# Attention stage: the softmax division moved from the weights to a head's output, with the reciprocals sent through DRAM to become a row

## The reference

```python
q = (query @ wq).reshape(bs, sq, N_Q_HEADS, D_K).transpose((0, 2, 1, 3))
...
q = _apply_rope(q, curr_seq_pos)
k = _apply_rope(k, curr_seq_pos)
raw = jnp.einsum('bhqd,bhkd->bhqk', q, k) / scale
masked = raw + mask[:bs, None, curr_seq_pos:curr_seq_pos + sq, :sk]
attn = jax.nn.softmax(masked, axis=-1)
out = jnp.einsum('bhqk,bhkd->bhqd', attn, v)
```

## Time and profile before

| | us |
|---|---|
| median of three runs | 3483.4 |
| lowest run | 3466.51 |
| the profiled execution | 3467.62 |
| its span, first to last instruction | 3465.7 |
| attention stage, from the first scores to the last matmul with v | 1004 to 1972 of the span |

### The profile page before, as it was taken

The page is one execution under the profiler, slowest core; times in us unless marked ns, Lnnn a source line. Parts: engine busy times, 40 slices in busy tenths (PEclk is TensorE's granted clock), DMA queues, the critical chain, the costliest instruction groups (busy, mean ns, idle before and its releaser), DMA issues. The chain is left out here.

```text
span 3465.7 us, 45672 instructions
## 1 busy us (share of the span) xinstructions
PE 3012.4 (87%) x14140; PEld 2414.5 (70%) x14144; DVE 2882.1 (83%) x4335; ACT 2154.2 (62%) x2742; POOL 911.5 (26%) x547
## 2 busy tenths in 40 slices
PE   5888858788769999999999899995656999999999
PEld 4777747566548888888888676763425777777787
DVE  7999969679759999999999799998584788888753
ACT  4777747567657777777777588884142565655531
POOL 3777746226111111111111055550000101101100
PEclk9999979899989999999999899997677999999999
DMA  3333432342331111111111244330022221212211
GB/s 111 128 112 116 133 133 91 122 139 91 128 119 53 55 46 61 49 59 49 58 49 49 88 130 132 121 109 31 0 97 67 68 67 61 85 61 67 73 49 52
DMA packets 170336, 286.81 MB, mean 83 GB/s; under 512 B 11712, under 2 KB 98752, under 8 KB 170176
## 3 DMA queue, kind: packets, MB, share of 16 engines
q1 hardware_dynamic: 160960, 268.24, 23.3%
q10 hardware_dynamic: 9216, 16.78, 1.3%
HBM read 196.64 MB, written 88.34 MB: 82 GB/s over the span
## 5 line engine op out<-in xcount | busy, mean ns | idle before, releaser
L898 ACT ACTIVATE at_pth<-at_t 128x512 fp32r<-128x512 f32 x512 | 282.1, 597 | 250.4 <-PE at_t L991 250.4
L941 DVE CUSTOM_DVE_ANT_0 at_sc<-at_s,at_mk 128x1024 f32<-128x1024 f32 x256 | 312.1, 1219 | 61.6 <-issue 40.0
L205 ACT ACTIVATE ff_nf_above<-ff_nf_raw,sharp 128x1024 f32<-128x1024 f32 x255 | 291.6, 1148 | 94.0 <-DVE ff_nf_val L220 74.4
L957 DVE TENSOR_TENSOR at_ptl<-at_t,at_pth 128x512 fp32r<-128x512 f32 x512 | 328.1, 682 | 1.1 <-ACT at_pth L898 1.1
L220 DVE SCALAR_TENSOR_TENSOR ff_nf_val<-ff_nf_above,ff_nf_val 128x1024 f32<-128x1024 f32 x238 | 308.2, 1295 | 21.2 <-ACT ff_nf_above L205 18.6
L205 ACT ACTIVATE pq_nf_above<-pq_nf_raw,sharp 128x1024 f32<-128x1024 f32 x240 | 263.1, 1113 | 98.9 <-DVE pq_nf_val L220 83.5
L205 ACT ACTIVATE ou_nf_above<-ou_nf_raw,sharp 128x1024 f32<-128x1024 f32 x240 | 267.3, 1117 | 77.8 <-DVE ou_nf_val L220 62.4
L888 ACT ACTIVATE at_pr<-at_sc,at_sm 128x1024 f32<-128x1024 f32 x256 | 295.2, 1153 | 21.8 <-DVE at_sm L944 15.1
L991 PE MATMUL at_t<-ident,at_pr 128*128 128x128 f32 x2048 | 273.1, 275 | 16.2 <-DVE at_ptl L957 16.0
L117 PE MATMUL ff_g<-yT_h,ff_guh 128*128 128x512 f32 x704 | 286.3, 407 | 0.0
L991 PEld LDWEIGHTS at_t<-ident,at_pr 128*128 128x128 f32 x2048 | 235.4, 140 | 67.4 <-DVE at_ptl L957 28.0
(11 more groups left out here) (210 smaller groups left out, 8091.0 us busy)
## 6 DMA issues: line engine op xcount, KB each, us to landing
ff_raw<-dq SPq DMA_DIRECT2D x63, 512.0 KB, 4.0
pq_raw<-in_L_xattn_wq SPq DMA_DIRECT2D x32, 512.0 KB, 5.4
q_d<-pq_res SPq DMA_DIRECT2D x32, 512.0 KB, 2.6
at_qraw<-q_d SPq DMA_DIRECT2D x64, 256.0 KB, 2.7
o_d<-at_ot ACTq DMA_DIRECT2D x64, 256.0 KB, 2.0
ou_oraw<-o_d SPq DMA_DIRECT2D x32, 512.0 KB, 3.9
ou_wraw<-in_L_xattn_wo SPq DMA_DIRECT2D x32, 512.0 KB, 4.0
pq_nf_raw<-in_L_ffn_w SPq DMA_DIRECT2D x16, 512.0 KB, 5.3
```

The source lines that it names most:

```text
L205: act.activation(self.above[:, (s + j) % 2, 0:width], self.raw[:, s, 0:width], ACT.Relu, bias=self.sharp[:, j:j + 1], scale=SHARP).then_in ...
L898: act.activation(pt[0][:, h % 2, j * HALF:(j + 1) * HALF, (n % QT) * P:(n % QT + 1) * P], t_ps[:, j], ACT.Copy).then_inc(t_hi.sem, 1)
L941: dve.tensor_tensor_reduce(sc[:, n % 2], s_ps[:, n % 2], mk[:, bb * QT + n % QT], 1.0, NEG, ALU.add, ALU.max, sm[:, n % 2, 0:1]).then_inc( ...
L957: dve.tensor_tensor(pt[1][sl], t_ps[:, j], f32(pt[0][sl]), ALU.subtract).then_inc(t_lo.sem, 1)
```

## The change

The row of `at_pr` stays undivided and PE turns it as soon as the exponentials are there. The mask pass gives the negated scores and their minimum `low`, which the exponentials take as bias with scale -1, so L944 is gone. The sums of a head's four quarters are collected in `sums` (128x4). Once per head, VectorE takes their reciprocals and turns them in 32x32 blocks (`invert`); SP stores them with four DMAs of 4 rows of 128 bytes each into a DRAM buffer `r_d` (512 numbers), and reads them back as one row broadcast to 128 partitions (`inv_row`, 128x512). GpSimd multiplies the head's output `at_ot` by it (`scale_out`), and SP, not ACT, stores the result.

```diff
+        INV_LAG = QT
+        ROW_LAG = QT + 2
...
+            def store_inverse(b, i, h):
+
+                sp.wait_ge(inv_turned.sem, inv_turned.done(head(b, i, h)))
+                for q in range(P // 32):
+                    sp.dma_start(r_d[h % 2].rearrange("(t q j) -> q t j", t=QT, j=32)[q],
+                                 invT[32 * q:32 * q + QT, h % 2]).then_inc(inv_out[h % 2], 16)
+
+
+            def load_inverse_row(b, i, h):
+                sp.wait_ge(inv_out[h % 2], written(b, i, h) + 64)
+                sp.dma_start(inv_row[:, h % 2], r_d[h % 2].rearrange('(a n) -> a n', a=1).broadcast_to((P, SQ))).then_inc(inv_in[h % 2], 16)
+
+            def store_out(b, i, h):
+                bb, hh = at(b, i, h)
+                sp.wait_ge(scaled.sem, scaled.done(head(b, i, h)))
+                sp.dma_start(o_d[bass.ds(hh, 1)].rearrange("a p n -> p (a n)")[:, bb * SQ:(bb + 1) * SQ],
+                             ot[:, h % 2]).then_inc(o_st[h % 2], 16)
+
             def do_step(b, i, n):
                 for kind, x in fetches(b, i, n):
                     fetch(b, i, kind, x)
-
+                for lag, act_on in ((INV_LAG, store_inverse), (ROW_LAG, load_inverse_row), (STORE_LAG, store_out)):
+                    if (n - lag) % QT == 0 and exists(b, i, n - lag):
+                        act_on(b, i, (n - lag) // QT)
...
+            def scale_out(b, i, h):
+                pool.wait_ge(inv_in[h % 2], passed(b, i, h) + 16)
+                pool.wait_ge(copied.sem, copied.done(head(b, i, h)))
+                pool.tensor_tensor(ot[:, h % 2], ot[:, h % 2], inv_row[:, h % 2], ALU.mult).then_inc(scaled.sem, 1)
+
             def do_step(b, i, n):
+                if (n - COPY_LAG) % QT == 0 and exists(b, i, n - COPY_LAG):
+                    scale_out(b, i, (n - COPY_LAG) // QT)
                 for kind, x in fetches(b, i, n):
...
-                act.wait_ge(maxed.sem, maxed.done(step(b, i, n)))
+                h, quarter = n // QT, n % QT
+                if quarter == 0:
+
+                    act.wait_ge(inverted.sem, inverted.free(head(b, i, h), 2))
+                act.wait_ge(masked.sem, masked.done(step(b, i, n)))
                 act.wait_ge(turned.sem, turned.free(2 * step(b, i, n) + 1, 4))
-                act.activation(pr[:, n % 2], sc[:, n % 2], ACT.Exp, bias=sm[:, n % 2, 1:2],
-                               accum_out=sm[:, n % 2, 2:3]).then_inc(expd.sem, 1)
+                act.activation(pr[:, n % 2], sc[:, n % 2], ACT.Exp, bias=low[:, n % 2:n % 2 + 1], scale=-1.0,
+                               accum_out=sums[:, h % 2, quarter:quarter + 1]).then_inc(expd.sem, 1)
...
-            def store_out(b, i, h):
-                bb, hh = at(b, i, h)
-                act.wait_ge(copied.sem, copied.done(head(b, i, h)))
-                act.dma_start(o_d[bass.ds(hh, 1)].rearrange("a p n -> p (a n)")[:, bb * SQ:(bb + 1) * SQ],
-                              ot[:, h % 2]).then_inc(o_st[h % 2], 16)
...
-                dve.wait_ge(masked.sem, masked.done(step(b, i, n)))
-                dve.tensor_scalar(sm[:, n % 2, 1:2], sm[:, n % 2, 0:1], -1.0, None, ALU.mult).then_inc(maxed.sem, 1)
-
-            def normalise(b, i, n):
-                dve.wait_ge(expd.sem, expd.done(step(b, i, n)))
-                dve.reciprocal(sm[:, n % 2, 3:4], sm[:, n % 2, 2:3]).then_inc(recipd.sem, 1)
-                dve.wait_ge(recipd.sem, recipd.done(step(b, i, n)))
-                dve.tensor_scalar(pr[:, n % 2], pr[:, n % 2], sm[:, n % 2, 3:4], None, ALU.mult).then_inc(normed.sem, 1)
+                dve.memset(turnstile[:, n % 2:n % 2 + 1], 0.0)
+                dve.tensor_tensor_reduce(sc[:, n % 2], s_ps[:, n % 2], mk[:, bb * QT + n % QT], -1.0, -NEG,
+                                         ALU.add, ALU.min, low[:, n % 2:n % 2 + 1]).then_inc(masked.sem, 1)
+
+            def invert(b, i, h):
+                dve.wait_ge(expd.sem, expd.done(step(b, i, QT * (h + 1) - 1)))
+                dve.reciprocal(inv[:, h % 2, 0:QT], sums[:, h % 2]).then_inc(inverted.sem, 1)
+                dve.wait_ge(inverted.sem, inverted.done(head(b, i, h)))
+                dve.wait_ge(inv_out[h % 2], written(b, i, h))
+                dve.transpose(invT[:, h % 2], inv[:, h % 2]).then_inc(inv_turned.sem, 1)
...
             def turn(b, i, n):
-                pe.wait_ge(normed.sem, normed.done(step(b, i, n)))
+                pe.wait_ge(expd.sem, expd.done(step(b, i, n)))
```

More of the change, by code:

```diff
@@ L715, in _, with attention_stage @@
                         last.then_inc(turned, 1)
-def attention_stage(nc, q_d, k_d, v_d, o_d, mask, ident):
+def attention_stage(nc, q_d, k_d, v_d, r_d, o_d, mask, ident):
     with ExitStack() as ctx:
@@ L745, in attention_stage @@
         ot = sb("ot", [P, 2, SQ], F32)
-        sm = sb("sm", [P, 2, 4], F32)
-        turnstile = sb("turnstile", [P, 1], F32)
+        low = sb("low", [P, 2], F32)
+        sums = sb("sums", [P, 2, QT], F32)
+        inv = sb("inv", [P, 2, 32], F32)
+        invT = sb("invT", [P, 2, 32], F32)
+        inv_row = sb("inv_row", [P, 2, SQ], F32)
+        turnstile = sb("turnstile", [P, 2], F32)
         s_ps = ps("s", [P, 2, SK])
@@ L759, in attention_stage @@
         masked = event("masked", 2)
-        maxed = event("maxed")
         expd = event("expd", 2)
-        recipd = event("recipd")
-        normed = event("normed")
+        inverted = event("inverted", 2)
+        cleared = sem("cleared")
+        inv_turned = event("inv_turned")
+        scaled = event("scaled", 2)
         turned = event("turned", 4)
@@ L779, in step, with passed @@
             return i * NS + (b * HQ * QT + n)
+        def passed(b, i, h):
+            return i * (16 * HP // 2) + 16 * (b * HQ // 2 + h // 2)
         def at(b, i, h):
@@ L785, in at, with written @@
             return b, i * HP + h
+        def written(b, i, h):
+            return i * (64 * HP // 2) + 64 * (b * HQ // 2 + h // 2 + 1)
         MIX_LAG = QT + 2
@@ L835, in do_step @@
                     fetch(b, i, kind, x)
+                for lag, act_on in ((INV_LAG, store_inverse), (ROW_LAG, load_inverse_row), (STORE_LAG, store_out)):
+                    if (n - lag) % QT == 0 and exists(b, i, n - lag):
+                        act_on(b, i, (n - lag) // QT)
+            for s in range(2):
+                sp.sem_inc(o_st[s], 16)
+                sp.sem_inc(inv_out[s], 64)
             for kind, x in FIRST:
@@ L840, in _ @@
             program(sp, do_step)
+            for s in range(2):
+                sp.wait_ge(o_st[s], 16 * (B * HQ // 2 + 1))
         @block.gpsimd
@@ L918, in do_step @@
                     exponentials(b, i, n)
-                for lag, act_on in ((COPY_LAG, copy_out), (STORE_LAG, store_out)):
-                    if (n - lag) % QT == 0 and exists(b, i, n - lag):
-                        act_on(b, i, (n - lag) // QT)
+                if (n - COPY_LAG) % QT == 0 and exists(b, i, n - COPY_LAG):
+                    copy_out(b, i, (n - COPY_LAG) // QT)
             expd.open(act)
             copied.open(act)
-            for s in range(2):
-                act.sem_inc(o_st[s], 16)
             for kind, x in FIRST:
@@ L929, in _, with mask_and_min @@
             program(act, do_step)
-            for s in range(2):
-                act.wait_ge(o_st[s], 16 * (B * HQ // 2 + 1))
         @block.vector
         def _(dve):
-            def mask_and_max(b, i, n):
+            def mask_and_min(b, i, n):
                 bb = at(b, i, n // QT)[0]
@@ L959, in do_step @@
             def do_step(b, i, n):
-                for lag, act_on in ((0, mask_and_max), (1, normalise), (2, turn_low)):
-                    if exists(b, i, n - lag):
-                        act_on(b, i, n - lag)
+                if exists(b, i, n):
+                    mask_and_min(b, i, n)
+                if (n - INV_LAG) % QT == 0 and exists(b, i, n - INV_LAG):
+                    invert(b, i, (n - INV_LAG) // QT)
+                if exists(b, i, n - 2):
+                    turn_low(b, i, n - 2)
             masked.open(dve)
+            inverted.open(dve)
+            dve.memset(inv[:], 0.0).then_inc(cleared, 1)
+            dve.wait_ge(cleared, 1)
             t_lo.open(dve)
@@ L1910, in build @@
         clear_stage(nc)
-        attention_stage(nc, q_d, k_d, v_d, o_d, mask, ident)
+        attention_stage(nc, q_d, k_d, v_d, r_d, o_d, mask, ident)
         output_stage(nc, o_d, wo, X, sharp, lambda k, e: unit(w[e % 2], k * 2 + (first_o + e // 2)),
```

9 lines of the change are left out of this document (5 added, 4 removed).

## The result

The changed kernel takes 3532.2 us (median of four, 3527.5 to 3540.7); the kernel before has a median of 3479.4 in the same comparison. The ratio is 1.0161, with an interval of 1.0144 to 1.0177: slower by 1.6%. The ratio compares fast executions alone, so the one of 10604.8 us among the four of the kernel before is not in it. The profiled execution took 3532.34 us, its span is 3530.4.

What follows compares the result with a forecast made beforehand. TensorE was taken to bound the plain attention step at 3.62 us, VectorE just behind. To 3467.62 us came +112 (late q), -28 (stalls given back) and +1 (last head): +85, 3553 us, range 3450 to 3625.

Steps and rivals of the forecast that it cites:

- What bounds the stage, and the gain: Attention stage: TensorE bounds the plain step at 3.62 us; a quicker VectorE gives back only the excess, -28 us together.
- the steps at a new k or v: Attention: pairs of steps stretched by 0.69 us at 15 key groups, 21 us, of which 19 was taken as gain.
- the four turns of the loop: Attention: 8.0 us of issue waits in four places, taken for the loop's turns; half, 4 us, was expected back.
- the first eight steps: Start of attention, where VectorE sets the pace: an estimated gain of 5 us, together with the last two steps.
- ScalarE and GpSimd at nothing: Attention: ScalarE gains nothing, and GpSimd's 64 added products, 82 us, are hidden except for the last head.
- the last head at +1: End of attention: GpSimd's product stands between copy and store of the last head, costing 1 us.
- The q load behind the stores: SyncE's queue: q's load waits behind the reciprocals' stores, reaches ScalarE late; TensorE loses 1.8 us per head, 112 us.
- The k load at 0: SyncE's queue: delays of the k and v loads hide behind q's and cost 0.
- The signs: Changed trace: L934 waits some 3 us, one step in four about 5.4, no stretch after k or v, issues 0.4 to 0.5 apart.
- Rival A: SyncE between reciprocal turn and q load: the queue hides the issues, four cost 0.2 us; 3452 us, chance 0.16.
- Rival B: SyncE's queue: the stores also hold up q's landing, 2 us later than taken; +124 us, 3677 us, chance 0.10.
- Rival C: Attention: VectorE was the true bound, so its saved time comes back; -270 us, 3200 us, chance 0.02.

Runs made afterwards that it cites:

- the repeat: A second profile of the changed kernel with SyncE's loads of q, k and v issued four steps earlier: attention stage 944.6 us, 940.1 the first time.
- the run without the detour: The changed kernel with loads four steps ahead, without reciprocal stores, row loads and GpSimd's product: stage 941.8 us, one execution of 3450.5 us.

## Why the prediction was right, and what was mis-sized

The direction, the mechanism and the range held; the median, 3532, is 21 below the 3553 foretold. The chances leaned to more than 2%, and the ratio is 1.6%.

That the total is only 21 off is in part luck. In the attention stage the sum has +84 (112 - 28) and 52 was measured, 32 less; outside it the sum has +1 and 12.8 was measured, of which 7 are the middle's clock and 2.7 lie ahead of attention, both not the change's.

*What bounds the stage, and the gain.* The prediction has "all that another engine can give back is what lies above 3.62", 28 us with the steps at the start and end. With q, k and v on time the stage is 27.7 us shorter than before, 23 in the repeat, and steps at a new k or v are no longer stretched (3.5 and 3.6 us where they were 4.3). The parts hold too, by the starts of the mask passes: the steps at a new k or v gave back 18.5 (19 foretold), the four turns of the loop 4.8 (4), the first eight steps 3.3 (5 with the last two). That the stretch came from the division pass meeting GpSimd's subtraction rests on the rows of before (1.66 for the pass beside L850); no run took that apart from the shorter step.

*ScalarE and GpSimd at nothing, the last head at +1.* Right: 0 in the stage by the run without the detour, 1.4 behind it. Not in the sum were the 1 to 3 us more that the output projection takes in every kernel with the detour.

*The q load behind the stores.* Right as a mechanism, shown from both sides: moved ahead, the loss is gone; made late in the kernel before, it comes. Step by step against the relay shown (from the start of the mask pass): transpose done at 1.65 (1.72 foretold), q issued at 3.21 (3.84), q copy started at 6.19 (6.69), `mix` at 9.10 (9.69). The term that was mis-sized is SyncE's part. The wake behind the transpose is 0.03, not the 0.18 taken from a wait on GpSimd, and four stores with q's address are 1.53, not 1.94: in the changed kernel a store of four rows is issued every 0.33 us in the median, not every 0.455 as the row of the 0.5 KB loads had it. The landing with ScalarE's start is 2.98, 0.13 longer than foretold. Over a head TensorE loses 1.2 to 1.3 us, not 1.8 (the stage is 79.6 us longer than with the loads ahead, 75.1 by the repeat, over 62 heads), so 75 to 80 us and not 112.

*The k load at 0.* True as a sum, and only because q is late in the same heads: the k copies do wait, 2.5 us each, and the step at a new k takes 4.3, but its head loses only 0.1 to 0.2 us more than the others. By itself the late k load costs 11 to 16 us.

*The signs.* ScalarE's wait on L934, 2.9 us in 61 heads, is there. The late step was put at about 5.4 and is 4.9 in the mean; the issues were put 0.4 to 0.5 apart and are 0.33. The step at a new v is no longer stretched (3.7); the step at a new k still is, by the late k copy, which was not foretold.

*Rival A* (issues hidden) had the direction of the error: the issues are cheaper than I took, but at 1.3 for four far from its 0.45. *Rival B* (the stores hold up the landing) is out: q lands in 2.5 at least and 2.8 in the median, 2.5 and 2.7 before, and with the stores on ScalarE's queue q is not late. *Rival C* (VectorE the bound) is out: 248 us less of VectorE's time gave 28.

The rule weighed, the Trainium skill's 50 ns of dispatch in "DMA: Bandwidth & Descriptors", section "Anatomy of one DMA — SWDGE (gpsimd) path", is given for DMAs that GpSimd issues. It does not hold for SyncE's issues here: four more tiny stores or three fewer move the next load by 0.32 to 0.34 us each. The prediction's "disagrees on both counts" goes too far: four issues in a row are not small beside a landing of 2.8 us, but one is. And the 2.7 that it sets beside them is the median of the q loads, not the landing of a load behind the four.

*The base.* 3467.6, the profiled execution of before, was a good one: it lies 9 to 12 us under the kernel's medians in the comparisons here (3476.7, 3478.3, 3479.4), and 10.3 us under the second profiled execution, all of it in the middle, where 2.4 GHz was granted for longer.

*The range.* Two figures of its working do not follow: with the 0.06 that it names, the transpose's low end takes off 0.14 and not 0.05, which makes the low sum +39 and not +44; and the forecast's own range starts at 3490, though 3467.6 + 44 is 3512. The 3532 measured lies above all of these.

## What to carry to other kernels

A queue that only issues loads may run many steps ahead of their use, and this lead is lost as soon as one wait for the current step is put into the same queue. Before adding a store there, list what stands behind it, and either move the loads up by as many steps as their buffers allow or give the store to another queue. Here a few lines that moved the loads turned +1.6% into -0.6%; the other queue brought the kernel level with the one before, since the k load stayed late. And look at which engine's instructions queue behind the consumer of the late transfer: ScalarE lost 3.6 us to a load that was needed only three steps later, because its copy stood first in the step.

## What the runs showed of the hardware beyond that

- A store of 4 rows of 128 bytes takes SyncE about as long to issue as a 256 KB load: such stores start 0.33 apart in the median, and q's load takes 0.33 to issue in the kernel before and 0.37 in the changed one.
- The row of 2 KB read to 128 partitions lands in 3.4 us, q's 256 KB from 128 different rows in 2.8:

```profile
at_qraw<-q_d SPq DMA_DIRECT2D x64, 256.0 KB, 2.8
at_inv_row<-r_d SPq DMA_DIRECT2D x64, 256.0 KB, 3.4
```

- VectorE's 32x32 transposes of 128x32 take 0.21 us, a reciprocal of 128x4 0.17.
- Behind a stretch almost without TensorE work at 1.2 GHz, the full clock came back at nearly the same place in two executions of one kernel (2436.0 and 2435.0), but then one had it for 80 us of the middle and the other for 55. That made 10 us of difference between two profiles of the same program, more than a third of the gain that this change had to offer.
